# A transformer kernel's first norm: where its sums, its constants and two groups of transposes stand

## The reference

```
x  = x + attn(layernorm(x), ...)        # attn = residual of mamba2 and a gated MLP, each behind an RMS norm
layernorm(x) = (x - mean(x)) / sqrt(var(x) + 1e-5)
rmsnorm(x, w) = x * rsqrt(mean(x*x) + 1e-5) * w
zxbcdt = rmsnorm(...) @ w_in.T           # 1024 -> z (1024), conv input (1536), dt (8)
xBC = silu(causal 4-tap conv of the conv input + bias);  dt = softplus(dt + dt_bias)
# then, in chunks of 128 tokens: running sums of dt*A, decays, attention-like products, states
```

## Time and profile before

| what | value |
|---|---|
| median of 3 runs (lowest, highest) | 2100.22 us (2099.84, 2101.30) |
| the profiled execution's own time | 2100.08 us |
| its span in the profile | 2098.1 us |
| PE, DVE, ACT busy, share of the span | 99%, 80%, 50% |
| mean granted clock of PE | 0.998 |
| the same shares from 10 to 20 us | PE 61%, DVE 85%, ACT 75% |

### The profile page before, as it was taken

The page is one execution under the profiler, slowest core; times in us unless marked ns, Lnnn a source line. Parts: engine busy times, 40 slices in busy tenths (PEclk is TensorE's granted clock), DMA queues, the critical chain, the costliest instruction groups (busy, mean ns, idle before and its releaser), DMA issues.

```text
span 2098.1 us, 26489 instructions
## 1 busy us (share of the span) xinstructions
PE 2074.9 (99%) x9230; PEld 1671.6 (80%) x9234; DVE 1677.2 (80%) x2526; ACT 1045.2 (50%) x1741; POOL 185.3 (9%) x296
## 2 busy tenths in 40 slices
PE   8999999999999999999999999999999999999999
PEld 4787778788888888888888855888888888888887
DVE  7887686697778888878979899977777776698885
ACT  5313244467777777774444466533333333444442
POOL 0001101101111112110000002010000100100000
PEclk9999999999999999999999999999999999999999
DMA  3151117649899999896430045544444443846101
GB/s 134 42 210 51 51 61 205 146 130 327 282 307 330 325 350 343 299 342 253 152 130 1 1 181 135 172 178 152 172 151 178 150 152 126 324 170 212 49 21 61
DMA packets 136434, 370.07 MB, mean 176 GB/s; under 512 B 16688, under 2 KB 27568, under 8 KB 132656
## 3 DMA queue, kind: packets, MB, share of 16 engines
q1 hardware_dynamic: 110640, 287.12, 39.8%
q0 software_dynamic: 25088, 80.23, 11.3%
q10 hardware_dynamic: 576, 1.05, 0.1%
HBM read 288.12 MB, written 84.41 MB: 178 GB/s over the span
## 4 chain that ended last, share of the span: by engine, by line
PE 91%; DVE 5%; ACT 1%; issue 1%; DMA 1%; SPq 0%; DVEq 0%; ACTq 0%
PE pair L1088 47%; PE pair L1136 24%; PE pair L858 7%; PE pair L851 5%; PE pair L1032 2%; PE pair L1098 1%; PE pair L970 1%; PE pair L991 1%; DMA sign_in_ab<-sign_spill 1%; PE pair L997 0%; DVE comb_lo L1903 0%; DVE ring_lo L1831 0%; PE pair L993 0%; DVE act_lo L2093 0%; DVE hs L2087 0%
## 5 line engine op out<-in xcount | busy, mean ns | idle before, releaser
L1088 PE MATMUL pair<-comb_hi,ring_hi 128*128 128x512 f32 x1456 | 566.8, 389 | 0.0
L1088 PE MATMUL pair<-comb_lo,ring_hi 128*128 128x512 f32 x1456 | 566.6, 389 | 0.0
L1088 PE MATMUL pair<-comb_hi,ring_lo 128*128 128x512 f32 x1456 | 566.6, 389 | 0.0
L1136 PE MATMUL pair<-inner_ring_a,ring_hi 128*128 128x512 f32 x1080 | 332.6, 389 | 0.0
L1088 PEld LDWEIGHTS pair<-comb_hi,ring_hi 128*128 128x128 f32 x1456 | 273.3, 188 | 58.2 <-issue 1.0
L1088 PEld LDWEIGHTS pair<-comb_hi,ring_lo 128*128 128x128 f32 x1456 | 273.3, 188 | 56.6
L1088 PEld LDWEIGHTS pair<-comb_lo,ring_hi 128*128 128x128 f32 x1456 | 273.3, 188 | 56.4
L1136 PEld LDWEIGHTS pair<-inner_ring_a,ring_hi 128*128 128x128 f32 x1080 | 202.7, 188 | 41.9
L1136 PE MATMUL pair<-inner_ring_a,ring_lo 128*128 128x512 f32 x540 | 210.1, 389 | 0.0
L1356 ACT ACTIVATE ring_hi<-ring_sum 128x512 fp32r<-128x512 f32 x160 | 100.5, 631 | 147.3 <-DVE ring_sum L1816 145.2
L1831 DVE TENSOR_TENSOR ring_lo<-raw_a,ring_hi 128x512 fp32r<-128x512 f32 x146 | 99.6, 686 | 54.5 <-ACT ring_hi L1356 52.9
(11 more groups left out here) (389 smaller groups left out, 3639.9 us busy)
## 6 DMA issues: line engine op xcount, KB each, us to landing
coeff_in<-f_gu SPq DMA_DIRECT2D x56, 512.0 KB, 5.3
coeff_in<-b_gu SPq DMA_DIRECT2D x56, 512.0 KB, 7.0
weights_raw<-w_mamba SPq DMA_DIRECT2D x44, 512.0 KB, 3.5
raw_a<-w_gu SPq DMA_DIRECT2D x28, 512.0 KB, 6.0
raw_a<-w_gu SPq DMA_DIRECT2D x56, 256.0 KB, 5.9
u_spill<-gate_a POOLq DMA_DIRECT2D x56, 256.0 KB, 5.0
coeff_in<-f_dn SPq DMA_DIRECT2D x28, 512.0 KB, 4.7
coeff_in<-b_dn SPq DMA_DIRECT2D x28, 512.0 KB, 6.7
```

The source lines that it names most:

```text
L1088: ins = pe.matmul(out, wt[:, slot, col], a, start=t in (0, 1, 3) and kk == 0 and n == 0, stop=kk == KH - 1 and n == 2, skip_group_check=True)
L1136: ins = pe.matmul(out, wt[:, slot, col], a, start=t in (0, 1, 3) and k == 0 and n == 0, stop=k == SC_PAIRS - 1 and n == 2, skip_group_chec ...
```

## The change

On PE the head gets 31 matmuls whose result is not used (`fill`), around the mean sums of half 0. The mean sums of half 1 are two matmuls and not four, since DVE adds pairs to fours first (`head_four`); so are the square sums of half 1. The square sums of half 0 go between the products of half 1. The eight transposes of dt are put two by two between the steps of block 4, and those of the running sums between the steps of block 9, whose waits now stand ahead of the block. `constants()` moves from the middle of the head to behind tile 9, ahead of `decay_rows()`; the two instructions for the dt weights stay in the head (`dt_weights`). ACT loads the table for the roots once, between the halves, and makes the first activation tile ahead of the second weight block. The other lines only follow the new counts.

```
+        def fill(count):
+            for _ in range(count):
+                pe.matmul(ps[3][:, HALF[0]], ones_bf[:, :], ones_bf[:, :].unsqueeze(1).to_broadcast([P, H // P, P]),
+                          start=True, stop=True)
         pe.wait_ge(s_const, 2)
-        for j in range(KT // 2):
-            head_mean(0, j)
+        fill(11)
+        head_mean(0, 0, 1, True, False)
+        fill(3)
+        head_mean(0, 1, 2, False, False)
+        fill(3)
+        head_mean(0, 2, 3, False, False)
+        head_mean(0, 3, 4, False, True)
+        fill(14)
         for k in range(KT):
             first_half(k, 0)
-            if k >= KT // 2:
-                head_mean(1, k - KT // 2)
-        head_var(0)
+            if k == KT - 2:
+                head_mean(1, 0, 7, True, False)
+        head_mean(1, 2, 10, False, True)
         for k in range(KT):
             first_half(k, 1)
-        head_var(1)
+            if k < KT // 2:
+                head_var(0, 4 + 2 * k, 11 + k, k == 0, k == KT // 2 - 1)
+        head_var(1, 4, 17, True, False)
+        head_var(1, 8, 20, False, True)
...
+        conv_block(2, 0, dt_tiles)
+        conv_block(2, 1)
+        for i in range(3, CONV_TILES // 2 - 2):
             conv_pair(i)
...
         pe.wait_ge(s_csx, 3)
+        conv_block(CONV_TILES // 2 - 2, 1, cs_tiles)
...
# ACT
         weights_hi(0, 0)
-        weights_hi(1, 1)
...
                 head_hi(b, k)
+                if b == 0 and k == 0:
+                    weights_hi(1, 1)
...
-                if b == 1 and k == 4:
+                if b == 1 and k == 6:
                     head_root(0)
...
+            if b == 0:
+                act.preload_act_table_set("natural_log_exp_and_others")
# DVE
+        def head_four(first, second):
+            dve.wait_ge(s_hpair, {(0, 1): 6, (2, 3): 9, (4, 6): 16, (8, 10): 19}[first, second])
+            TT(xbc[:, first, HALF[1]], xbc[:, first, HALF[1]], xbc[:, second, HALF[1]], ALU.add).then_inc(s_hpair, 1)
...
-            if k >= KT // 2:
-                head_pair(1, k - KT // 2)
-        for j in range(KT // 2):
-            head_square_pair(0, j)
-        constants()
+            if 3 <= k < KT - 1:
+                head_pair(1, k - 3)
+            if k in (4, 6):
+                head_four(k - 4, k - 3)
+        dt_weights()
         head_centre(1, 0)
         head_centre(1, 1)
         for k in range(KT):
             if k + 2 < KT:
                 head_centre(1, k + 2)
             head_lo(1, k)
-            if k == 1:
+            if k < KT // 2:
+                head_square_pair(0, k)
+            if k == 4:
                 head_var(0)
             if k >= 3 and k % 2 == 1:
                 head_square_pair(1, (k - 3) // 2)
+            if k == 6:
+                head_four(4, 6)
         head_square_pair(1, KT // 2 - 1)
+        head_four(8, 10)
         head_rsqrt(0)
...
         n = CONV_TILES - 2
+        constants()
         decay_rows()
```

More of the change, by code:

```diff
@@ L845, in _, with block_mm @@
     def _(pe):
-        def block_mm(out, wi):
+        def block_mm(out, wi, small=None):
             for k in range(KT):
+                if small is not None:
+                    small(k)
                 for n, (w, a) in enumerate(((WH, ah), (WH, al), (WL, ah))):
@@ L863, in _, with head_mean, head_var @@
         pe.sem_inc(s_stage, 1)
[L866 to L869, removed]
+        def head_mean(b, tile, sums, first, last):
+            pe.wait_ge(s_hpair, sums)
+            ins = pe.matmul(ps[2][:, HALF[b]], ones_mean[:, :], xbc[:, tile, HALF[b]], start=first, stop=last)
+            if last:
                 ins.then_inc(s_hm, 1)
-        def head_var(b):
-            for j in range(KT // 2):
-                pe.wait_ge(s_hpair, KT + b * (KT // 2) + j + 1)
-                pe.matmul(ps[3][:, HALF[b]], ones[:, :], xbc[:, 4 + 2 * j, HALF[b]],
-                          start=j == 0, stop=j == KT // 2 - 1).then_inc(s_hvar, 1)
+        def head_var(b, tile, sums, first, last):
+            pe.wait_ge(s_hpair, sums)
+            pe.matmul(ps[3][:, HALF[b]], ones[:, :], xbc[:, tile, HALF[b]], start=first, stop=last).then_inc(s_hvar, 1)
         def first_half(k, b):
@@ L920, in _, with dt_tiles @@
         conv_pair(1)
+        def dt_tiles(k):
+            for t in range(2 * k, min(2 * k + 2, NC)):
+                ins = pe.matmul(ps[3][:, t * 2 * HEADS:(t + 1) * 2 * HEADS], dt_rows[:, t * P:(t + 1) * P],
+                                shp[0:2 * HEADS, 1, 0:2 * HEADS], start=True, stop=True)
+                if t == NC - 1:
+                    ins.then_inc(s_dtm, 1)
         pe.wait_ge(s_dts, 1)
         pe.wait_ge(s_ht, BATCH + 1)
[L923 to L928, removed]
+        conv_block(2, 0, dt_tiles)
+        conv_block(2, 1)
+        for i in range(3, CONV_TILES // 2 - 2):
             conv_pair(i)
@@ L933, in _, with cs_tiles @@
         pe.matmul(ps[2][:, 320:384], ones[:, :], a_all[:, :, :], start=True, stop=True).then_inc(s_dtm, 1)
-        conv_pair(CONV_TILES // 2 - 2)
+        conv_block(CONV_TILES // 2 - 2, 0)
+        def cs_tiles(k):
+            for t in range(2 * k, min(2 * k + 2, NC)):
+                ins = pe.matmul(ps[3][0:PARTS_K, t * P:(t + 1) * P], cs_wide[:, t, :], ident, start=True, stop=True)
+                if t == NC - 1:
+                    ins.then_inc(s_dtm, 1)
         pe.wait_ge(s_csx, 3)
-        for t in range(NC):
-            ins = pe.matmul(ps[3][0:PARTS_K, t * P:(t + 1) * P], cs_wide[:, t, :], ident, start=True, stop=True)
-        ins.then_inc(s_dtm, 1)
+        conv_block(CONV_TILES // 2 - 2, 1, cs_tiles)
         conv_pair(CONV_TILES // 2 - 1)
@@ L1200, in _ @@
         feed_forward(W_END[0] - 4, W_END[0] - 2)
[L1201 removed]
+        ctx_var(bank(1), x_square_a, range(KH), HEAD_SUMS, (), 0)
         feed_forward(W_END[0] - 2, W_END[0])
@@ L1220, in _ @@
         column_sums(1, bank(3))
-        ctx_var(bank(7), x_square, range(KH), 2 * KT + KH, (), 0)
+        ctx_var(bank(7), x_square, range(KH), HEAD_SUMS + KH, (), 0)
         pe.wait_ge(s_mc, 2)
@@ L1248, in _ @@
         pe.wait_ge(s_xt, 6)
-        ctx_var(bank(7), x_square, range(KH), 2 * KT + 2 * KH, (), 0)
+        ctx_var(bank(7), x_square, range(KH), HEAD_SUMS + 2 * KH, (), 0)
         pe.wait_ge(s_rlo, 2)
```

23 lines of the change are left out of this document (12 added, 11 removed).

## The result

| | before | after |
|---|---|---|
| median (lowest, highest), 7 runs each | 2100.15 us (2099.37, 2101.30) | 2107.9 us (2106.10, 2114.98) |
| ratio, 95% interval | | 1.0042 (1.0033 to 1.0052) |
| span of the profiled execution | 2098.1 | 2105.8 |
| mean granted clock in it | 0.998 | 0.998 |

The kernel became 7.7 us slower, and its runs lie further apart than before's. The forecast was 2102.7, with a range from 2097.5 to 2106.0, and was wrong. The 7.7 is the difference of the medians; the ratio and its interval put it at 6.9 to 10.9 us.

The account below looks back on a forecast made before the run. PE, busy 99% of the span, was taken to bound the kernel, its head lead counting only if DVE comes earlier too. Block 4's 2.1 plus the first chunk's 0.4 gave 2.5 us and 2102.7 us, range 2097.5 to 2106.0.

Parts of the forecast that it names:

- Half 0 and the constants: Head and behind tile 9: DVE centres at 10.75 and gains 2.8 us by half 1; constants take 3.1 behind tile 9.
- Half 1: Second half of the head: DVE's longer queue puts the first tile at 56.8, so block 2 starts at 58.0, as before.
- the first rival: Clock falls in PE's 2.7 us idle time between the halves, delaying tiles and variance sums 1.7 to 2.0: 2104.6; 20%.
- Block 4: PE idles from 79.8 to 82.0 for low weights, then spread transposes cost 1.85: +2.1 us at block 5.
- The first chunk: First chunk stage: the last tile is taken at 179.2, PE arrives at 178.8, a new wait of 0.4 us (0 to 1.0).
- The sum: Whole kernel: 2.1 at block 4 plus 0.4 at the first chunk stage make 2.5 us, predicting 2102.7.
- Rival 2: Blocks 4 and 9: the spread transposes cost nothing, 3.6 us less in all, 2099.0; 10%.
- rival 3: Head: DVE keeps pace and takes the first tile at 53.3, so PE keeps its 1.3 us: 2098.9; 10%.

Follow-up runs that it names:

- with the constants in the gap: Changed kernel with the gap between the halves filled, block 4's transposes in front and the constants back in that gap: 2102.2 us, ratio 1.0011.
- with the squares back: Changed kernel with half 0's four square sums and their matmuls back between the halves and block 4's transposes in front: 2098.4 us, ratio 0.9992.
- with two loads: Changed kernel with square sums back between the halves, block 4's transposes in front, and the root table loaded ahead of each root: 2098.3 us.
- the first combination: Changed kernel, square sums between halves, block 4's transposes in front, constants between tiles 8 and 9, half 1's variance copy ahead of low weights: 2097.2 us, ratio 0.9983.

## Why the prediction was wrong

**Half 0 and the constants: right, a little late.** First centring forecast at 10.75, measured 11.32 (10.78 to 11.41 in all profiles with the filled head); that of half 1 at 29.8, measured 30.57. The fill kept the clock, as said.

**Half 1: right in its mechanism, wrong about its clock.** The step that failed is "Half 1", which priced PE's tiles and sums at the fast clock. With the gap filled, the forecast of 58.0 for block 2 is met at 58.5. In the changed kernel it was 60.7: the fall cost 1.6, and 0.5 more is the later start of that profile's head. This was the first rival, put at 20% and priced at 1.7 to 2.0. Its doubt, that the gap was shorter than the 3.77 us of the earlier trace rows, did not save the changed kernel. The Trainium skill (TensorE: Matmul & The Clock Gate, Part 1) calls the activity window free-running; by that the same gap may or may not meet a fall. The runs agree, since the gap of 2.6 us was followed by a fall in two profiles of the changed kernel and by none in that with the transposes in front.

**Block 4: two things missed.** The prediction wrote that "PE idles from 79.8 to 82.0", and did not apply its own first rival to this second gap. The clock fell behind it as well: from block 2 to the small sums took 72.1 us with that fall and 70.6 without, 1.5 of the clock's part. And the transposes, taken at 1.85 with ends of 0 and 2.1, cost 4 x 0.77 = 3.1, beyond the upper end: the price was read from matmuls with 128 rows, and these have 16. Together, without the clock: 2.15 of wait, 3.1 of groups, less 1.9 in one piece, 3.3 where 2.1 was forecast, and 3.2 in the profile of the run with only the squares back (125.5 - 54.9, against 67.4).

**The first chunk: right.** 0.35 of new wait, forecast 0.4.

**The sum.** Forecast 2.1 + 0.4; in the changed kernel's profile over that of the kernel before: the head without the clock +1.0 (forecast 0; 0.6 of it is that DVE's first centring came at 11.32 and not at 10.75), block 4 without the clock +3.2, the first chunk +0.6, the two falls +1.6 and +1.5, 7.9 in all. Even without the falls the forecast is too low, by the transposes above all: with both idle times filled the median is 4.2 over the kernel before, not 2.5. Rival 2 (transposes free) and rival 3 (DVE keeps pace; it took the first tile at 57.1 with the gap filled, not at 53.3) are out. What the prediction had right, and what was the heart of it, is that DVE's queue eats up what the constants and the earlier mean give: putting the four sums back into the idle time gives 3.1 us, or 4.0 between two kernels without a fall in their profiles.

## What to carry to other kernels

Before work is moved out of a gap, look at whether the gap closes: an idle engine that still waits for the same thing costs nothing to fill, and the work costs its whole time where it goes. Where a change moves small work from in front of a wait to behind it, count the wait as bare, and then ask what the clock does behind it; price such a gap every time it occurs, not once. A mean granted clock that differs between executions of one kernel by 0.001 is worth up to 2 us in 2100, where the engine does not wait anyway, and a filler in the right gap takes out both the loss and the scatter. Two kernels with the same mean clock can still pay differently for it: ask where the stretches stand. And before two profiles are compared by position, look at whether they already differ ahead of the change.

## What the hardware showed that was not expected

- Idle times of PE of 2.64 and 2.15 us are followed by 3.4 us at 0.50 (1.2 GHz) in some executions and in others not (2.64 with the transposes in front, 2.12 and 2.10 with only the squares back), and the stretch can be twice as long (6.8 us behind 2.11 us of idle time, and behind 3.77 in the kernel before with block 4's transposes spread). 3.4 us at 0.50 cost 1.5 to 1.6 us where PE sets the pace, 6.8 us cost 3.0.
- A piece of sixteen passes of 16-column transposes (1.95 us, PE busy all through) was followed by a fall in the profiles of five kernels (with the transposes in front, with the constants in the gap, with the squares back, with two loads, the first combination), and by none in the kernel before and the three others that have it. The stretches began 0.2 to 1.1 us behind the end of the piece; what decides it was not tried.
- Four passes of a transpose with 16 rows and 16 columns cost 0.77 us between matmuls of 512 columns and 0.47 in one piece (1.89 / 4 in the kernel before, whose block 4 they stand in front of); with 128 rows they cost 0.47 between matmuls. Why the 16-row ones are dearer there was not tried.
